# Per-head multiply-and-sum with an accumulator output in place of one wide multiply and one wide reduction, on one Trainium2 core

## The reference, cut to what matters

```
q, k, v = (x @ Wq + bq), (x @ Wk + bk), (x @ Wv + bv)        # each n x 8 x 64
logits  = einsum('ehd,ehd->eh', q[rows] / 8, k[cols]) + att_bias
p       = exp(logits - segment_max(logits)[rows])
y       = segment_sum(p[:, :, None] * v[cols]) / segment_sum(p)
out     = y @ Wo + bo
```

## Time and profile before

| | us |
|---|---|
| three runs | 3325.85, 3326.24, 3329.14 |
| median | 3326.24 |
| span of the profiled execution (first to last instruction) | 3328.5 |
| the runs' highest, which its span is nearest to | 3329.14 |
| edge loop in it, from about 1161 to 2932 | 1771 |

### The profile page before, as it was taken

The page is one execution under the profiler, slowest core; times in us unless marked ns, Lnnn a source line. Parts: engine busy times, 40 slices in busy tenths (PEclk is TensorE's granted clock), DMA queues, the critical chain, the costliest instruction groups (busy, mean ns, idle before and its releaser), DMA issues.

```text
span 3328.5 us, 51387 instructions
## 1 busy us (share of the span) xinstructions
PE 2913.6 (88%) x11922; PEld 1712.5 (51%) x12048; DVE 2900.1 (87%) x8850; ACT 2181.1 (66%) x7642; POOL 2204.1 (66%) x2509
## 2 busy tenths in 40 slices
PE   6897889887988169999999999999999999989999
PEld 4554445554554025555555555555555555555555
DVE  9897777776776279999999999999999999998886
ACT  6432222222221039999999999999999999964443
POOL 0377777777777647777777777777777777741111
PEclk9898888888888589999999999999999999999998
DMA  6344333333332487888888888788888888831221
GB/s 209 80 136 107 106 99 103 103 106 100 103 103 85 166 286 256 255 253 254 257 256 260 253 261 253 254 255 256 255 256 255 260 253 258 256 100 66 76 76 69
DMA packets 259197, 615.22 MB, mean 185 GB/s; under 512 B 69755, under 2 KB 80327, under 8 KB 258642
## 3 DMA queue, kind: packets, MB, share of 16 engines
q0 software_dynamic: 144832, 443.72, 42.3%
q1 hardware_dynamic: 107718, 155.40, 15.5%
q10 hardware_dynamic: 6348, 12.80, 1.1%
HBM read 550.28 MB, written 61.49 MB: 184 GB/s over the span
## 4 chain that ended last, share of the span: by engine, by line
DVE 28%; POOL 25%; issue 20%; PE 15%; DMA 8%; DVEq 2%; another core or an unknown queue 1%; ACT 0%; ACTq 0%; SPq 0%; POOLq 0%
POOL rec_scratch L631 21%; DMA big<-kv_scratch,small 8%; DVE big L1396 7%; DVE small L1289 6%; DVE big L1283 5%; PE banks L1920 5%; POOL big L652 2%; PE banks L1899 2%; PE banks L1982 2%; DVE big L1009 2%; PE banks L1847 1%; POOL small L659 1%; PE banks L1755 1%; DVE big L1014 1%
## 5 line engine op out<-in xcount | busy, mean ns | idle before, releaser
L815 ACT ACTIVATE big<-big,small 128x65 f32<-128x65 f32 x6564 | 1604.3, 338 | 4.8
L652 POOL DMA_INDIRECT big<-kv_scratch,small x832 | 842.3, 1012 | 407.6 <-DVE small L1289 286.5
L631 POOL DMA_INDIRECT rec_scratch<-big,small x782 | 770.6, 985 | 342.2 <-issue 237.7
L1899 PE MATMUL banks<-big,small 128*128 128x260 f32 x3328 | 897.9, 393 | 87.0 <-POOL small L659 45.6
L1847 PE MATMUL banks<-big,small 128*128 x1664 | 873.3, 607 | 34.6 <-DVE big L1283 16.1
L1899 PEld LDWEIGHTS banks<-big,small 128*128 128x128 f32 x3328 | 598.8, 190 | 522.3 <-issue 249.7
L1755 PE MATMUL banks<-big 128*128 128x512 f32 (+1 forms) x1176 | 611.1, 668 | 22.3 <-DVE big L999 22.3
L1396 DVE SCALAR_TENSOR_TENSOR big<-big,loS,banks 128x520 f32 x832 | 611.5, 735 | 5.4 <-PE banks L1899 4.4
L1283 DVE TENSOR_TENSOR big<-banks,big 128x512 f32<-128x512 f32 x832 | 558.8, 672 | 44.7 <-PE banks L1847 24.1
L659 POOL TENSOR_SCALAR small<-iotaF,small 128x128 f32<-128x128 f32 x832 | 525.9, 632 | 50.6 <-PE banks L1899 25.1
L1289 DVE TENSOR_REDUCE small<-big 128x8 f32<-128x512 f32 x832 | 548.8, 664 | 0.0
(11 more groups left out here) (263 smaller groups left out, 2720.4 us busy)
## 6 DMA issues: line engine op xcount, KB each, us to landing
rowR<-lo_rows SPq DMA_DIRECT2D x97, 256.0 KB
big<-src_rows SPq DMA_DIRECT2D x97, 256.0 KB, 3.5
big<-in_x_dram SPq DMA_DIRECT2D x96, 256.0 KB, 2.8
big<-kv_scratch,small POOLq DMA_INDIRECT x832, 5.2
rec_scratch<-big,small POOLq DMA_INDIRECT x782
kv_scratch<-big SPq DMA_DIRECT2D x48, 260.0 KB
q_scratch<-big SPq DMA_DIRECT2D x48, 256.0 KB
kv_scratch<-big SPq DMA_DIRECT2D x48, 256.0 KB
```

The lines of the kernel that those rows point to most:

```text
L631: e.indirect_dma_start(recd, bass.IndirectOffsetOnAxis(ap=ridx[:, c % 4, j:j + 1], axis=0), rec[:, 8 * c + j, :], None).then_inc(s_sc[c % ...
L652: e.indirect_dma_start(KV[:, vat(t):vat(t) + YW + D], None, KVd, bass.IndirectOffsetOnAxis(ap=recB[b_ % 4][:, t % 16, 9:10].bitcast(i32), ...
L815: ins = e.activation(heads(Vr(t), h, h + 1), heads(Vr(t), h, h + 1), ACT.Copy, scale=ph[:, h:h + 1])
L1899: ins = e.matmul(YB[t % 2][:, i, :], oh[t % 4], Vr(t)[:, 260 * i:260 * i + 260], start=True, stop=True)
```

## The change

- `pr` and `rd` are gone. `kq(t, half)` does both for four heads: for each head one SCALAR_TENSOR_TENSOR of 64 columns, (K x Q) with the factor 1.0 between, in place over K, whose accumulator output is the head's sum. `kq(s, 0)` stands where `pr(s)` stood and `kq(s, 1)` where `rd(s-1)` stood; `rd(s-1)` ahead of `ya` in steps with `at == 0` is gone too. So tile `s` is both multiplied and summed in step `s`.
- The semaphore `s_pr` is gone. `expand_q(t)` and the last stage's first operations wait on `s_rd` in its place, with the same numbers.
- The one-hot row in `scale_parts` is a tensor_tensor of `iotaF` with the column of `llb` broadcast to 128, instead of a tensor_scalar with that column as a per-partition scalar.
- ACT's program is not touched by the diff: it scales all eight heads of V in steps below `LAST` and does so before too.

```
-            def pr(t):
+            def kq(t, half):
 
                 q.wait_ge(s_q1, t + 1)
                 q.wait_ge(s_kv[t % 8], 16 * (t // 8 + 1))
-                e.tensor_tensor(Kr(t), QB[t % 2], Kr(t), ALU.mult).then_inc(s_pr, 1)
-
-            def rd(t):
-
-                q.wait_ge(s_pr, t + 1)
                 q.wait_ge(s_x2, t // 16 - 1)
-                e.tensor_reduce(Lr[t // 16 % 2][:, t % 16, :], Kr(t).rearrange("p (h d) -> p h d", d=64), AX.X, ALU.add).then_inc(s_rd, 1)
+                for h in range(4 * half, 4 * half + 4):
+                    k_ = Kr(t)[:, 64 * h:64 * h + 64]
+                    ins = e.scalar_tensor_tensor(k_, QB[t % 2][:, 64 * h:64 * h + 64], 1.0, k_, ALU.mult, ALU.mult,
+                                                 accum_out=Lr[t // 16 % 2][:, t % 16, h:h + 1])
+                if half:
+                    ins.then_inc(s_rd, 1)
...
-                e.tensor_scalar(Aoh[0:8, :], iotaF[0:8, :], llb[0:8, max(b_ - 1, 0):max(b_ - 1, 0) + 1], None, ALU.is_equal).then_inc(s_bd, 1)
+                e.tensor_tensor(Aoh[0:8, :], iotaF[0:8, :], llb[0:8, max(b_ - 1, 0):max(b_ - 1, 0) + 1].broadcast_to([8, 128]), ALU.is_equal).then_inc(s_bd, 1)
...
-                if at == 0:
-                    rd(s - 1)
...
                 if s < T:
-                    pr(s)
+                    kq(s, 0)
...
-                if 1 <= s < T and at != 0:
-                    rd(s - 1)
+                if s < T:
+                    kq(s, 1)
...
                 q.wait_ge(s_oh, t // 4 + 1)
-                q.wait_ge(s_pr, t - 1)
+                q.wait_ge(s_rd, t - 1)
```

More of the change, by code:

```diff
@@ L306, in build @@
         s_kv = sems("s_kv", 8)
-        s_oh, s_q1, s_pr, s_rd, s_lb, s_x2 = sem("s_oh"), sem("s_q1"), sem("s_pr"), sem("s_rd"), sem("s_lb"), sem("s_x2")
+        s_oh, s_q1, s_rd, s_lb, s_x2 = sem("s_oh"), sem("s_q1"), sem("s_rd"), sem("s_lb"), sem("s_x2")
         s_f1, s_d1, s_zm, s_zs, s_za, s_cf = sem("s_f1"), sem("s_d1"), sem("s_zm"), sem("s_zs"), sem("s_za"), sem("s_cf")
@@ L582, in _ @@
             q.wait_ge(s_rd, T)
-            q.wait_ge(s_pr, T)
             q.wait_ge(s_q1, T)
@@ L1904, in f_yT @@
                 q.wait_ge(s_yn, w + 1)
-                q.wait_ge(s_pr, T)
+                q.wait_ge(s_rd, T)
                 q.wait_ge(s_yT, w)
```

## The result

The changed kernel takes 3289.82 us (median of 4 runs, 3288.61 to 3291.39), the kernel before 3326.05 beside it (4 runs, 3318.67 to 3329.14). The ratio is 0.9892, 95% interval 0.9878 to 0.9905: 36 us or 1.1% faster. In a few executions the granted clock was lower throughout and the time 400 to 1500 us longer (the kernel before twice in the experiments, `row_pool_heads` once); they are left out of every ratio, though not of the medians.

What follows compares the result with a forecast made beforehand. DVE was taken as the bound with ACT close second, ACT taking over at 33.0 us per block. -25 in the loop, +8 stalls, -1 at the start made -18 against the 3328.5 span, 3310.5; given as 3309, range 3300 to 3350.

Steps and rivals of the forecast that it cites:

- In the loop nothing waits long for gathers, so that is 0 there: Gathers in the loop: being able to start nearly a step earlier gains 0; at the loop's start it gains 1 us.
- At most 33 us of it can reach the end: Loop: ACT's whole idle time, 33.0 us, caps what DVE's gain can take off the end.
- Stalls that stay: Loop: DVE and ACT don't hide each other fully, 0.15 us per block, +8 us in the sum.
- DVE's work: DVE per block in the loop: 33.5 - 1.0 - 0.2 + 0.3 = 32.6 us.
- The pair: DVE in each step: a 64-column instruction with its accumulator read takes 0.142 us, eight take 1.14 instead of 1.20.
- a dear pair: Rival: 64-column pairs from PSUM pay a fixed part, slower from 0.149 us per pair; 3350 at 0.153; chance 0.17.
- a slow queue: Rival: DVE's issue rate leaves 0.1 us before every `ya`, block 34.2, time 3362; chance 0.08.
- The one-hot row: `scale_parts` on DVE: the two-tensor form takes 0.20 us instead of 0.42, a gain of 0.2 per block.
- The register load: DVE's queue, once per block: a 1.10 us load is less covered after the change and costs 0.3 us.
- ACT takes over: Loop: ACT becomes the bound at 33.0 us per block, -10 to -26 us, 3300 to 3316; the forecast case, chance 0.47.
- PE's wait: `expand_q` on PE waits for sums instead of the product, 0.5 us later; cost 0, as PE has 1.4 to spare.
- POOL's wait on the sums: Gathers on POOL: 202.6 us in 300 waits for the sums, expected to be about gone.

Runs made afterwards that it cites:

- `row_pool_heads`: Changed kernel with the one-hot row on POOL and DVE scaling four heads of V in one tile of 32 instead of ACT; 3515.32 us, ratio 0.992.
- `late_release`: Changed kernel with each gather waiting until one tile more has been summed; 3539.37 us, ratio 0.9962 to the kernel before on its own chip.
- `act_less`: Changed kernel with ACT leaving one of V's eight heads unscaled in steps below `LAST`; 3514.84 us, ratio 0.9901 to the kernel before on its own chip.
- `dve_less`: Changed kernel with head 7's instruction covering 8 columns instead of 64; 3504.65 us, ratio 0.9886 to the kernel before on its own chip.
- `one_hot_alone`: Kernel before with only the one-hot row changed to the two-tensor form; 3550.30 us, ratio 1.0001 to the kernel before on its own chip.

## Why the prediction was wrong

**The step that failed** is "In the loop nothing waits long for gathers, so that is 0 there". What it rested on was POOL's wait for the sums, read as harmless, and the absence of a large wait of DVE. But the release was the last link of a ring that was nearly tight. The trace of before had it in two places. DVE's waits for gathered data were 20.2 us in 19 waits, of which the prediction counted one, the 3.99 at the start; they fell to 4.1 with the change. (Nor has DVE's chain "no gaps", as it says: by the earlier trace rows it was idle for 13.9 us.) And the starts of one line over all blocks show a block of 33.70 on average, mostly between 33.3 and 34.6, though its work is always the same. I took one block, 33.52. `late_release` measures the term: 18.6 us in the loop, of which about 4 in the first two blocks. It had 0 in the sum, and 1 at the start.

**"At most 33 us of it can reach the end"** was no ceiling. ACT's need was sized right: 33.0 forecast, 33.05 now (32 activations in 7.66 to 7.67). A block of before had 33.70, so ACT's slack was 0.65 per block, 33 us over the loop, which is what the earlier trace rows say; the prediction's own sum used 0.5 x 50.8 = 25 of them, from its one block. What the earlier trace rows leave out are the first two blocks, from before ACT had filled: they gave 8.7 more.

**Stalls that stay**, +8 us in the sum, came out near nothing: DVE idles 0.07 per block and ACT has no wait at L776. With two engines this close I expected them to hinder each other; `act_less` and `dve_less`, at 33.07 and 33.05, against 33.09 with both at full work, show that they hardly do in the changed kernel.

**DVE's work** was forecast at 32.6 and is 33.0 to 33.05. Its terms:
- The pair: 0.142 forecast, 0.144 measured, which is 0.26 per block over 128 pairs; and the product and sum that it replaces cost 1.193 over the loop instead of the 1.20 of one step, 0.11 per block. The most sensitive term was right to 2 ns, so the rivals with a dear pair and with a slow queue fell. By the figure in the Trainium skill ("VectorE: DVE Perf Modes", the section on the TRN2 errata) eight pairs were an estimated 1.53 us; they take 1.16 in the step shown. Its 120 fixed cycles from PSUM don't show in this trace.
- The one-hot row: 0.2 of gain forecast, none measured. The price of 0.20 is met in `one_hot_alone` and missed in the changed kernel, where most rows cost 0.475 just behind the start of a gather; the old form costs 0.42 in that place. By the Trainium skill ("GPSIMD Engine Reference", section 1, Specifications) VectorE contends with GpSimd for memory if it has two inputs there or runs in a two-port mode. The dear rows are what that rule would give; the cheap ones of `one_hot_alone`, with a gather at the same distance, it leaves unexplained. What else decides is open: no run took POOL's gather away at that moment while the row stayed on DVE.
- The register load: 0.3 forecast. From L1380's start to the next start it is 0.67 against 0.61 before, so 0.06 was lost. The load begins 0.55 us ahead of L1380 (median of 51), under the last four pairs, and its other 0.55 lies under L1380; the prediction had let the pairs cover less of it.
- `ya` costs 0.668 instead of 0.663, 0.08 per block, which I didn't have; why is open.

Added to the forecast 32.6: 0.26 + 0.11 + 0.2 - 0.24 + 0.08 = 0.41, so 33.0.

Together they make the tie: not "ACT takes over", but both at 33.0 to 33.05. The forecast's direction, its block of 33.0 and ACT's wait ahead of L777 that vanishes were right. Its gain per block was too small since it started from 33.5 and not from 33.7, and since it kept 0.15 for stalls.

**Right at nothing:** PE's wait (`PE banks L1844 <- DVE big L1285`, 29.5 us from 1400 to 2800, none of it passed on to DVE), the issue rate of 17 instructions per step, the removal of `s_pr`.

**POOL's wait on the sums** didn't vanish as I wrote (130.1 us in 191 waits from 1400 to 2800). No wait of DVE or ACT shows that it costs anything now.

**Summing up the 38 us of the loop:** about 18 from the earlier release (first two blocks included), about 20 from cheaper products and sums up to ACT's bound. The second is the difference from the kernel before to `late_release`, whose window equals that of before only to 0.1 us; by times it is 11. Two readings of the traces agree with it. DVE's waits for gathered data fell by 16.1 us (20.2 to 4.1), and 11.7 of them came back in `late_release` (15.8 up to its loop's end). And if each of a block's sixteen steps is taken at its median length, from product to product over steps 64 to 799, the kernel before adds up to 33.51 and the changed one to 33.1, while their mean blocks are 33.70 and 33.09: 0.4 per block is work, 0.2 is stalls, and `late_release` has 33.12 and 33.37. Part of the 8.7 of the first two blocks is scatter, as said above. The split is known to some 10 us.

## What to carry to other kernels

Before a price list, list the starts of one line over all iterations, and add up all waits of the bound engine by what ended them, small ones too. Here, iterations of equal work had unequal lengths because a ring of waits was nearly tight, and an edit that moved a release by a step was worth about as much as the arithmetic. Undo the timing and the arithmetic separately, and push the timing one step the wrong way: if that costs 12%, the kernel stood next to an edge. When two engines end level, only work that leaves both (here for a third with time to spare) moves the end.

## What the runs showed of the hardware

- Start to start, a DVE product with accumulator output costs 0.09 us at 16 columns and 0.144 at 64; the plain product costs 0.60 at 512. In `dve_less` a pair of 8 columns costs 0.086. That is about 0.07 to 0.08 fixed and 1.03 to 1.04 ns per column, and eight pairs (1.155 per tile) were cheaper than two wide instructions (1.193).
- A comparison of 128 columns on 8 partitions costs DVE 0.20 or, 0.32 us after a gather has begun on POOL, up to 0.475 with two tensors and 0.42 with a scalar column. The same distance to a gather gave 0.20 in one kernel and 0.475 in another; why is open.
- An indirect gather of one tile lands 5.2 to 5.3 us (median) after it starts on POOL, and in the kernel before it starts 0.3 us (median) behind the sum that releases it. With two steps and a `ya` between release and use both kernels fall to the same 37.61 us per block, which stretches that window to 5.8 us (median).
